# Graph attention on one core: the last half tile in three loads, and fewer dependent VectorE steps in the last group

## The reference

```python
h = input @ W
e = (h @ a1)[:, None] + (h @ a2)[None, :]
e = jnp.where(e > 0, e, ALPHA * e)
e = jnp.where(adj > 0, e, NEG)
attention = jax.nn.softmax(e, axis=1)
x = _layernorm(x + elu(attention @ h), axis=-1)
```

## Time and profile before

| | us |
|---|---|
| median of three runs | 710.41 |
| lowest, highest | 709.22, 713.4 |
| the profiled execution's own time | 709.52 |
| its span (first to last instruction) | 707.7 |
| PE, DVE, ACT, POOL busy | 549.5, 480.7, 524.2, 444.0 |
| mean granted TensorE clock | 0.894 |

### The profile page before, as it was taken

How to read it: one execution, slowest core, us unless ns; L and a number is a source line. 1 busy time by engine, 2 the same in 40 slices (tenths; PEclk the granted TensorE clock), 3 DMA queues, 4 the chain that set the end, 5 groups by cost and what they waited for, 6 DMA issues and landing times.

```text
span 707.7 us, 11837 instructions
## 1 busy us (share of the span) xinstructions
PE 549.5 (78%) x3034; PEld 343.5 (49%) x3083; DVE 480.7 (68%) x2058; ACT 524.2 (74%) x423; POOL 444.0 (63%) x676
## 2 busy tenths in 40 slices
PE   0867898686787878988987777788787877798885
PEld 0323455453455545555555454455554544565554
DVE  2374577877666676766776767766667767656886
ACT  0846778777787878787877787878787878778741
POOL 2015377776666765666776676666776676667773
PEclk9979998999999997988999999989999999878998
DMA  8999999999999999999999999999999999999645
GB/s 346 333 413 426 426 426 424 427 426 425 426 426 426 429 427 427 427 426 427 426 428 430 426 426 425 429 425 428 429 426 428 425 427 426 427 424 428 274 119 151
DMA packets 34598, 285.57 MB, mean 404 GB/s; under 512 B 5528, under 2 KB 13872, under 8 KB 18064
## 3 DMA queue, kind: packets, MB, share of 16 engines
q1 hardware_dynamic: 29024, 276.83, 93.6%
q0 software_dynamic: 5120, 8.42, 3.3%
q10 hardware_dynamic: 432, 0.07, 0.1%
HBM read 283.18 MB, written 4.19 MB: 406 GB/s over the span
## 4 chain that ended last, share of the span: by engine, by line
DMA 67%; ACT 11%; PE 10%; issue 5%; DVE 4%; POOL 1%; SPq 1%; ACTq 0%; POOLq 0%; DVEq 0%
DMA adj_sb<-in_adj 65%; ACT adj_squared L618 11%; PE fold L752 6%; DMA a_sb<-in_L_gnn_a 2%; POOL edge_row L383 1%; PE misc L794 1%; PE x_att_ps L817 1%; PE fold L748 1%; SPq L421 1%; DVE spread L395 0%; PE small L767 0%; DVE top_map L1000 0%; DVE dot L1111 0%; POOL spread L401 0%; PE x_att_ps L820 0%
## 5 line engine op out<-in xcount | busy, mean ns | idle before, releaser
L618 ACT ACTIVATE adj_squared<-adj_sb 128x4096 bf16<-128x4096 int32 x128 | 462.7, 3615 | 117.8 <-DMA adj_sb<-in_adj 116.9
L752 PE MATMUL fold<-adj_sb,bit_ident 128*128 128x512 bf16 x993 | 301.5, 448 | 9.7 <-DMA adj_sb<-in_adj 5.3
L543 POOL DMA_INDIRECT nb<-in_x,index x160 | 165.2, 1032 | 93.7 <-issue 60.4
L752 PEld LDWEIGHTS fold<-adj_sb,bit_ident 128*128 128x128 bf16 x1024 | 110.3, 108 | 154.0 <-issue 67.2
L1000 DVE MAX8 top_map<-fold 128x8 f32<-128x512 f32 x128 | 89.4, 699 | 72.4 <-PE fold L752 69.5
L748 PE MATMUL fold<-col_no,ident_bf 128*128 128x512 bf16 x112 | 47.9, 428 | 111.0 <-DMA adj_sb<-in_adj 110.8
L383 POOL TENSOR_SCALAR edge_row<-row_iota,edge_in 128x128 f32<-128x128 int32 x186 | 127.4, 699 | 0.0
L401 POOL TENSOR_TENSOR spread<-edge_row,edge_w 128x384 f32<-128x384 f32 x60 | 54.9, 934 | 83.2 <-DVE edge_w L1156 83.2
L748 PEld LDWEIGHTS fold<-col_no,ident_bf 128*128 128x128 bf16 x128 | 15.9, 124 | 133.6 <-issue 90.1
L516 POOL TENSOR_SCALAR empty_diag<-ident,counts 128x128 f32<-128x128 f32 x64 | 39.2, 618 | 54.3 <-DVE counts L1036 33.3
L817 PEld LDWEIGHTS x_att_ps<-spread,nb 128*128 128x128 f32 x372 | 52.8, 205 | 8.1 <-issue 2.3
(11 more groups left out here) (154 smaller groups left out, 615.1 us busy)
## 6 DMA issues: line engine op xcount, KB each, us to landing
adj_sb<-in_adj SPq DMA_DIRECT2D x127, 2048.0 KB, 16.2
out<-x_sb SPq DMA_DIRECT2D x2, 1536.0 KB, 7.8
nb<-in_x,index POOLq DMA_INDIRECT x160, 6.2
adj_sb<-in_adj SPq DMA_DIRECT2D x2, 1024.0 KB, 15.0
out<-x_sb SPq DMA_DIRECT2D x4, 128.0 KB, 2.8
out<-x_sb SPq DMA_DIRECT2D x1, 384.0 KB, 8.0
out<-x_sb SPq DMA_DIRECT2D x2, 64.0 KB, 1.6
W_sb<-in_L_gnn_W ACTq DMA_DIRECT2D x1, 64.0 KB, 7.9
```

Source lines behind the costliest of these rows:

```text
L543: nc.gpsimd.indirect_dma_start(out=nb_of(j, g)[:, c, :], out_offset=None, in_=x[:, :], in_offset=bass.IndirectOffsetOnAxis(ap=index[:, g, ...
L618: nc.scalar.activation(adj_squared[:, h % 2, :], adj_sb[:, h % LOAD_SLOTS, :], ACT.Square, accum_out=half_sum[:, h:h + 1]).then_inc(square ...
L752: last = nc.tensor.matmul(fold[:, h % LOAD_SLOTS, :], bit_ident[:, b, :], adj_low[:, h % LOAD_SLOTS, b * FOLD:(b + 1) * FOLD, 0], start=Fa ...
```

## The change

Three edits, all of which act in the last group alone; the loop and the other groups run the instructions of before.

1. The second part of the last half, 2048 columns, is loaded in two parts of 1024. PE waits for the one ahead of bit 4 and for the other ahead of bit 6; ACT waits for both.
2. In the last group `lists` scales the picked values by 2^8 in one instruction (`peel[0]`) beside the rounding (`top_int`), masks the exponent of that (`top_lead`) beside the column, subtracts it (`peel[1]`) beside `from_base`, and masks both peels in one instruction of 64 columns with a mask of four exponent bits. The constants of the threshold and of the row numbers are those of the new codes. One memset of one column is added at the start.
3. In the last group `scores` adds the own score and takes the minimum with `cap` in one instruction per tile, ahead of the leaky ReLU.

```diff
@@ load
-                        parts = 2 if is_final(i, g) and h == HALVES - 1 else 1
+                        cuts = LAST_CUTS if is_last_half(i, h) else (0, BITS)
...
+        LAST_CUTS = (0, BITS // 2, 3 * BITS // 4, BITS)
@@ square_half
-                        act.wait_ge(rest_loaded, 16)
+                        for landed in rest_loaded:
+                            act.wait_ge(landed, 16)
@@ fold_half
-                        if is_last_half(i, h) and b == BITS // 2:
-                            pe.wait_ge(rest_loaded, 16)
+                        if is_last_half(i, h) and b in LAST_CUTS[1:]:
+                            pe.wait_ge(rest_loaded[LAST_CUTS.index(b) - 1], 16)
@@ lists
+                    if is_final(j, g):
+                        nc.vector.tensor_scalar(peel[:, 0, :], maps, LIFT / UNIT, LIFT * (FOLD // 2), ALU.mult, ALU.add)
+                        v.after(nc.vector.tensor_scalar(top_int[:], maps, 1.0 / UNIT, float(FOLD // 2),
+                                                        ALU.mult, ALU.add))
+                        nc.vector.tensor_tensor(top_lead[:], peel[:, 0, :].bitcast(i32),
+                                                exp_bits[:, 0:1].to_broadcast(flat), ALU.bitwise_and)
+                        v.after(nc.vector.tensor_tensor(top_col[:], top_int[:], col_bits[:, 0:1].to_broadcast(flat),
+                                                        ALU.bitwise_and))
+                        nc.vector.tensor_tensor(peel[:, 1, :], peel[:, 0, :], top_lead[:].bitcast(fp32), ALU.subtract)
+                        v.after(nc.vector.tensor_tensor(from_base[:], half_base[:].rearrange("p q s -> p (q s)"),
+                                                        top_col[:], ALU.subtract))
+                        v.after(nc.vector.tensor_tensor(
+                            lead[:].rearrange("p k s -> p (k s)"), peel[:].rearrange("p k s -> p (k s)").bitcast(i32),
+                            kept_bits[:, 0:1].to_broadcast([P, PEELS * 2 * PAIR * 8]), ALU.bitwise_and))
...
-                    v.after(nc.vector.tensor_scalar(is_code[:], sent[:, :, 0:SLOTS], float(NO_CODE), None, ALU.is_gt))
+                    v.after(nc.vector.tensor_scalar(is_code[:], sent[:, :, 0:SLOTS],
+                                                    float(LAST_NO_CODE if is_final(j, g) else NO_CODE), None, ALU.is_gt))
@@ scores
+                    if is_final(j, g):
+                        for t in range(PAIR):
+                            last = nc.vector.scalar_tensor_tensor(
+                                score[:, t, :], t_row_ps[:, t, :], s_all[:, last_tile(t):last_tile(t) + 1],
+                                cap[:, g, t, :], ALU.add, ALU.min)
+                        v.after(last)
+                        v.after(nc.vector.scalar_tensor_tensor(score_l[:], score[:], ALPHA, score[:],
+                                                               ALU.mult, ALU.max))
+                        top_scores(slots)
+                        return
```

More of the change, by code:

```diff
@@ L81, in graph_attention @@
     NO_CODE = COL_0 - N - FOLD
+    LIFT = 2.0 ** 8
+    KEPT_BITS = 0b00010111 << 23
+    LAST_COL_0 = FOLD * (16 + BITS - 1) + HALF
+    LAST_NO_CODE = LAST_COL_0 - N
     EDGES = CHUNKS * P // PAIR
@@ L120, in graph_attention @@
         exp_bits = sb("exp_bits", [P, 1], i32)
+        kept_bits = sb("kept_bits", [P, 1], i32)
         half_base = sb("half_base", [P, 2 * PAIR, 8], i32)
@@ L151, in graph_attention @@
         rest_code = sb("rest_code", [P, 2 * PAIR * 8], fp32)
+        peel = sb("peel", [P, PEELS, 2 * PAIR * 8], fp32)
+        top_lead = sb("top_lead", [P, 2 * PAIR * 8], i32)
         from_base = sb("from_base", [P, 2 * PAIR * 8], fp32)
@@ L257, in graph_attention @@
         loaded = [sem(f"loaded{s}") for s in range(LOAD_SLOTS)]
-        rest_loaded = sem("rest_loaded")
+        rest_loaded = [sem(f"rest_loaded{k}") for k in range(2)]
         chunk_gathered = [sem(f"chunk_gathered{c}") for c in range(CHUNKS)]
@@ L415, in step @@
                             sp.wait_ge(folded, i * HALVES + (h + 1 - LOAD_SLOTS))
-                        parts = 2 if is_final(i, g) and h == HALVES - 1 else 1
-                        size = HALF // parts
-                        for k in range(parts):
-                            lo = (h % 2) * HALF + k * size
-                            tile = adj_tiles[bass.ds(i * BODY + h // 2, 1), :, lo:lo + size]
-                            nc.sync.dma_start(adj_sb[:, h % LOAD_SLOTS, k * size:(k + 1) * size],
+                        cuts = LAST_CUTS if is_last_half(i, h) else (0, BITS)
+                        for k, (b, end) in enumerate(zip(cuts, cuts[1:])):
+                            lo, hi = (h % 2) * HALF + b * FOLD, (h % 2) * HALF + end * FOLD
+                            tile = adj_tiles[bass.ds(i * BODY + h // 2, 1), :, lo:hi]
+                            nc.sync.dma_start(adj_sb[:, h % LOAD_SLOTS, b * FOLD:end * FOLD],
                                               tile.rearrange("o p c -> (o p) c")).then_inc(
-                                                  rest_loaded if k else loaded[h % LOAD_SLOTS], 16)
+                                                  rest_loaded[k - 1] if k else loaded[h % LOAD_SLOTS], 16)
                     if first(i) and g == 0:
@@ L958, in _ @@
                 nc.vector.memset(exp_bits[:], EXP_BITS)
+                nc.vector.memset(kept_bits[:], KEPT_BITS)
                 nc.vector.memset(col_bits[:], FOLD - 1)
@@ L1012, in lists @@
[L1012 to L1018 removed]
+                    maps = top_map[:].rearrange("p q s -> p (q s)")
@@ new lines, in lists @@
+                    if is_final(j, g):
[12 more added lines that the diff above has]
+                            kept_bits[:, 0:1].to_broadcast([P, PEELS * 2 * PAIR * 8]), ALU.bitwise_and))
+                    else:
+                        v.after(nc.vector.tensor_scalar(top_int[:], maps,
+                                                        1.0 / UNIT, float(FOLD // 2), ALU.mult, ALU.add))
+                        v.after(nc.vector.tensor_tensor(top_col[:], top_int[:], col_bits[:, 0:1].to_broadcast(flat),
+                                                        ALU.bitwise_and))
+                        nc.vector.tensor_tensor(from_base[:], half_base[:].rearrange("p q s -> p (q s)"), top_col[:],
+                                                ALU.subtract)
+                        v.after(nc.vector.tensor_tensor(top_code[:], top_int[:], top_col[:], ALU.subtract))
+                        v.after(nc.vector.tensor_tensor(lead[:, 0, :], top_code[:].bitcast(i32),
+                                                        exp_bits[:, 0:1].to_broadcast(flat), ALU.bitwise_and))
+                        v.after(nc.vector.tensor_tensor(rest_code[:], top_code[:], lead[:, 0, :].bitcast(fp32),
+                                                        ALU.subtract))
+                        v.after(nc.vector.tensor_tensor(lead[:, 1, :], rest_code[:].bitcast(i32),
+                                                        exp_bits[:, 0:1].to_broadcast(flat), ALU.bitwise_and))
```

17 lines of the change are left out of this document (3 added, 14 removed).

## The result

The changed kernel takes 721.43 us (median of 4 runs, 719.64 to 722.88), the kernel before, run beside it on the same chip, 710.40 (4 runs): a ratio of 1.0145, with a 95% interval of 1.0125 to 1.0165. The forecast was 709.6 within 708.4 to 711.3; the median lies 10.1 us over the upper bound, more than three times the width of that range.

The account below looks back on a forecast made before the run. The prediction took DMA, 67% of the span, as the bound. Its terms 0.20 + 0.21 + 0 = 0.41 us, taken as 0.4 from a middle of 710.0, gave 709.6 us, range 708.4 to 711.3.

Parts of the forecast that it names:

- the first one: Whole kernel: the loop reading `adj` stays as it is, so only the 36.9 us behind the last load can change.
- Three loads: Last half: PE runs without a stop and DVE's MAX8 loses its idle time; gain 0.16 to 0.24 us, taken 0.20.
- Rival B: PE's wait ahead of bit 6: the last part lands later, kernel 0.5 us slower at 710.5; chance 0.12.
- Lists: Last group, first instruction to `cand`: pairs without waits cut 1.46 us to 1.25, a gain of 0.21.
- rival A: VectorE pays per instruction, not per wait: `lists` stays at 1.46 us, only 0.2 us gained, 709.8; chance 0.08.
- Scores: Last group, up to the maximum: 0.64 us becomes 0.55, but hidden behind PE's sums; term 0, at most 0.1.
- What moves along: Tail: the 0.41 us passes through PE, POOL's copy (idle 0.58 us, 0.17 left) and the last gathers.
- rival D: Tail: smaller slack or a DVE wait loses 0.1 to 0.3 us, or `scores` gains 0.1; 709.5 to 709.9; chance 0.13.
- The clock: Tail: TensorE's clock falls; at half clock PE's 5.4 us of the chain double, giving 715; chance 0.02.
- same: Whole time: no change beyond the measurable 0.5% (3.6 us), chance 0.94; faster 0.03, slower 0.03.

Follow-up runs that it names:

- tiles_only: The kernel before with only the change's three new tiles declared, unused, in the changed kernel's places: 720.05 us, ratio 1.0138.
- after: The changed kernel with all three edits, against the kernel before: 721.43 us, ratio 1.0145.
- nb_32: The kernel before with a 32-byte pad ahead of `nb` and another behind, so `nb` begins 32 past a multiple of 512: 719.21 us, ratio 1.0138.
- shift_384: The kernel before with only `peel` and `top_lead` declared, unused, so `nb` begins 384 past a multiple of 512: 721.94 us, ratio 1.0153.
- no_split: The changed kernel without the three-part load; the other two edits and the new tiles stay: 719.87 us, ratio 1.0128 against the kernel before.
- before: The kernel without the change, the reference for the others: 710.40 us beside the changed kernel.
- shift_32: The kernel before with only `kept_bits` declared, unused, so `nb` begins 32 past a multiple of 512: 722.10 us, ratio 1.0174.
- nb_alone: The kernel before with 32 bytes ahead of `nb` and 480 behind, so only `nb` changes its place within 512: 720.93 us, ratio 1.0137.
- nb_256: The kernel before with a 256-byte pad ahead of `nb` and another behind, so `nb` begins 256 past a multiple of 512: 711.36 us, ratio 1.0005.
- adj_only: The kernel before with `adj_sb` and `nb` on multiples of 512, `x_sb` left 128 past one: 707.24 us, ratio 0.9950.
- all_512: The kernel before with `x_sb`, `adj_sb` and `nb` all on multiples of 512: 703.56 us, ratio 0.9898.
- after_aligned: The changed kernel with a 96-byte pad putting `nb` back on a multiple of 512: 709.22 us, ratio 0.9977 against the kernel before.
- best: The changed kernel with `x_sb`, `adj_sb` and `nb` all on multiples of 512: 702.08 us, ratio 0.9881 against the kernel before.
- split_only: The kernel before with only the last half loaded in three parts: 711.32 us, ratio 1.0016.
- tiles_last: The changed kernel with its three new tiles declared behind all others: 710.58 us, ratio 1.0003 against the kernel before.
- again: The changed kernel run once more, unaltered: 720.00 us, ratio 1.0118 against the kernel before.

## Why the prediction was wrong

**The step that failed** is the first one: "The middle of the kernel is the reading of `adj`, and the change leaves the loop as it is, so only the stretch behind the last load can change." The instructions of the loop were left, but not the addresses that they write to. `tiles_only` has not one instruction more than the kernel before and costs 1.0138. The stretch that the prediction dismissed holds 9 us of loss, some twenty times the 0.41 that it worked out with care elsewhere. It had also priced what the change adds in instructions, DMAs and a memset, and never the declarations, which the excerpt of the diff ahead of it leaves out.

**Three loads:** 0.16 to 0.24 forecast. Shown where PE comes ahead of the landing, and nothing where it comes late. In `after` DVE, from the first of the two MAX8 on (timeline):

```profile
684.79 1.28 DVE L1011 MAX8 top_map<-fold 128x8 f32<-128x512 f32 x2
686.11 0.29 DVE L1019 TENSOR_SCALAR peel<-top_map 128x32 f32<-128x32 f32 x1
686.21 0.22 DVE L1020 TENSOR_SCALAR top_int<-top_map 128x32 int32<-128x32 f32 x1
686.46 0.19 DVE L1022 TENSOR_TENSOR top_lead<-peel,exp_bits 128x32 int32<-128x32 int32 x1
686.57 0.18 DVE L1024 TENSOR_TENSOR top_col<-top_int,col_bits 128x32 int32<-128x32 int32 x1
...
687.12 0.22 DVE L1029 TENSOR_TENSOR lead<-peel,kept_bits 128x64 int32<-128x64 int32 x1
687.37 0.23 DVE L1046 SCALAR_TENSOR_TENSOR cand<-lead,from_base 128x64 f32<-128x64 int32 x1
```

The two MAX8 now follow each other with no idle time, 1.28 us in all; before, they took from 671.09 to 672.64, 1.55. But in `after` PE came to the last half when all of it had landed, and kernels without the split in which PE came late as well have 1.28 too: `nb_32` and `shift_384`, which have no edit at all, and `no_split`:

```profile
681.37 1.28 DVE L1011 MAX8 top_map<-fold 128x8 f32<-128x512 f32 x2
```

So there the gain is not the split's. Where PE opens the last half 0.9 to 1.1 us ahead of the last packet's end, the two MAX8 take 1.45 to 1.57 without the split (`before`, `tiles_only`, `shift_32`, `nb_alone`, `nb_256`, `adj_only`, `all_512`) and 1.28 with it (`after_aligned`, `best`). Both kernels show the forecast mechanism, PE's eight products in one piece with no wait (`after_aligned` here):

```profile
669.33 1.97 PE L763 MATMUL fold<-adj_sb,bit_ident 128*128 128x512 bf16 x8
```

Part of it is given back at once: behind two MAX8 with no wait between them the first instruction of `lists` lasts 0.29 us where it lasted 0.18, and the old chain then takes 1.56 (`nb_32`) or 1.57 (`split_only`, below) and not 1.46. The prediction had no such term. Rival B, the later landing, did not happen: no kernel with the split has a wait of PE in the last half.

```profile
672.96 1.29 DVE L1001 MAX8 top_map<-fold 128x8 f32<-128x512 f32 x2
674.28 0.29 DVE L1007 TENSOR_SCALAR top_int<-top_map 128x32 int32<-128x32 f32 x1
```

**Lists:** 1.25 us forecast from the first instruction to `cand`; 687.37 - 686.11 = 1.26 above, and 1.26 in `no_split`, `tiles_last` and `after_aligned` as well, 1.27 in `again`. `best` has 1.45, because its first pair took 0.48 and 0.41 us and not 0.29 and 0.22; why is not known. Pairs start 0.10 and 0.11 apart. With the old chain it is 1.57 in `split_only` and 1.45 in `nb_256` and `all_512`. Under like conditions, two MAX8 with no wait ahead, the gain is thus 1.57 - 1.26 = 0.31 and not 0.21. The rule of the Trainium skill (page "VectorE: DVE Perf Modes", section "The DRAIN you can't avoid") that removing waits gains nothing, rival A, does not hold for these small instructions: eight instructions before and after, 1.46 or 1.57 against 1.26. The section also says that a next instruction that is not held starts earlier, and with that the trace agrees: 0.10 and 0.11 us behind the other where a step with a wait takes 0.22.

**Scores:** 0.55 us forecast, 0.60 measured (0.61 in `after_aligned`, 0.73 in `tiles_last`), as from the pair of reads from PSUM to the next step it is 0.39 and not 0.33. PE's sums follow on one another in `after_aligned` with no gap ahead of `small<-share`, so the 0.04 gained there is hidden, as said.

**What moves along.** From the opening of the last half to the first of the last gathers it was 681.77 - 669.36 = 12.41 us; in `after_aligned` it is 681.14 - 669.11 = 12.03, so 0.38 arrives there. The split has little part in it: it is 12.03 in `no_split` as well, and 12.34 in `split_only` against 12.33 to 12.41 in the kernels without any edit. POOL's copies stand at 678.01 and 678.14 with no idle time between, where there were 0.58 us: the slack was used up entirely, not down to 0.17.

```profile
678.01 0.20 POOL L535 COPY half_sum_all<-half_sum 128x4 f32<-128x4 f32 x1
678.14 0.19 POOL L541 COPY counts_all<-counts 128x4 f32<-128x4 f32 x1
...
681.14 1.06 POOL L553 DMA_INDIRECT nb<-in_x,index  x1 [1.25 <-DVE index L1131]
```

To the end of the span it is 707.0 - 669.11 = 37.89 us against 38.34: 0.45 gained, forecast 0.41; in `after` it is 37.95. These two are the best cases. In `again`, `no_split` and `best`, whose clock stayed at 1.00 in this stretch too, it is 38.21, 38.28 and 38.30, hardly less than the 38.27 to 38.35 of the kernels without any edit and with a full clock in the tail. The last gathers start as early in `again` and `no_split` as in `after`, and the gain is lost behind them, where DVE comes to the scores of the group ahead and waits for PE's `send_scores`. That wait is in these three, and neither in `after` and `after_aligned` nor in the kernels without any edit; first `after_aligned`, then `best`:

```profile
684.48 0.15 DVE L1172 TENSOR_TENSOR score<-misc,s_all 128x20 f32<-128x20 f32 x1
```

```profile
677.52 0.18 DVE L1173 TENSOR_TENSOR score<-misc,s_all 128x20 f32<-128x20 f32 x1 [0.17 <-PE misc L806]
```

From the opening of the last half this instruction starts at 15.37 us in `after_aligned` and at 15.61 to 15.72 in the three. So rival D, a gain that does not arrive, did happen, in three of the five executions that have the edits to `lists` and `scores` and a full clock in the tail, and at a wait that the prediction had not named; PE's products for it start at the same 13.66 to 13.76 us in all five, and what makes DVE wait for them in some is not known. `tiles_last` has the same 12.02 us up to that gather (683.11 - 671.09), but 38.71 to the end of its span: its clock fell once more, to 0.71 over 680 to 685 us, and there six products from `spread` take 1.53 us where they take 0.94.

So the forecast of the tail was right in the mechanisms on DVE. That its 0.41 came out in two executions is in part luck: `lists` gave more than its term, the split less, and what arrives at the end depends on a wait outside the sum. It is too small to be shown by times: 0.9977 (0.9961 to 0.9993) for `after_aligned` is the most that can be said for it, and `tiles_last` has 1.0003.

**The clock** was given 0.02, because "PE's work behind the load is the same". The fall came ahead of the last halves, a place that this argument leaves out. What it cost here (4.3 us in `after`, some 2.4 in the tail of `all_512` and of `nb_256`, 0.5 to 0.8 in that of `tiles_last`) shows that a chance for it belonged in the range on the upper side. It falls in kernels without any edit as well, so it scatters every measurement here and does not come from the edits alone.

**The chances** had 0.94 on "same" because every case considered lay in the tail. No rival said that the change might touch the loop after all. A ratio of 1.0145 with an interval of 1.0125 to 1.0165 is beyond the 0.5% that the prediction took for the limit of what can be told apart, on the slower side, to which it gave 0.03.

## Why a place costs time

Three numbers from the runs can be put side by side. `nb` takes 160 gathers of 128 rows, 20480 rows of 512 bytes. Off a multiple of 256 it costs 720.93 - 711.32 = 9.6 us of 16 engines (`nb_alone`), 7.5 ns of one engine per row. `x_sb` takes 8192 rows of 512 bytes, and 128 off it costs 707.24 - 703.56 = 3.7 us, 7.2 ns per row. `adj_sb` takes 16384 rows of 16 KB, and 128 off it costs 711.29 - 707.24 = 4.1 us, 4.0 ns per row. So it is a price per row that does not grow with the row's length, and it does not grow with the distance from the multiple either (32, 384 and 416 are alike). These are estimates, worked out from differences of medians. The packets' own records bear them out: for `x_sb` (116.5 - 88.5) / 4 = 7.0 ns per row, and for `adj_sb` a packet over 1 us away from any gather's takes 614.2 ns in `after_aligned` and 611.4 in `best`, 2.8 ns per row.

The Trainium skill has a rule that fits (page "DMA: Bandwidth & Descriptors", section "How a descriptor splits into AXI transactions"): a transfer is cut at 256-byte boundaries, so one that does not begin on such a boundary needs one piece more. By it a row of 512 bytes goes from two pieces to three wherever between two boundaries it begins, and a row of 16 KB from 64 to 65. The runs agree in both: one price for 32, 384 and 416, none for 256. They agree less in the beats that the section counts, 16 for the aligned row and by its way of counting 17, 20 and 21 for 32, 384 and 416 past: the runs do not tell these three apart. The section speaks of reads, and here it is the writes that are off; that the cut is the cause is argued from this fit and not shown. Tried were 32, 128 and 160 bytes past a multiple of 256, and none; other places, and rows of other lengths, were not.

## What to carry to other kernels

A declaration is a part of a change: whatever stands behind a new tile moves, and if the target of a small-row transfer is among it, the kernel can lose 1.4% of its time with no instruction changed, as here, where the DMA engines are full. Put new tiles last, or pad so that targets of transfers begin on a multiple of 256 bytes, and compare the GB/s of the untouched stretch before reading anything else. And before saying that a stretch cannot change, ask what it shares with the rest: addresses, engines and the clock.

## What the runs showed of the hardware that was not expected

- The place of a transfer's target within SBUF counts: 427 against 421 GB/s for 32 bytes (`nb_alone`), and 429 with all targets on multiples of 512.
- The cost of the gathers' place appears in the records of the other stream: 16-KB packets of `adj` are 644 ns long in place of 617 while the badly placed gathers fly, and unchanged outside, while the share of the gathers' own queue in such a round is 10.0% in both.
- The first instruction of `lists`, of 32 columns on VectorE, behind two MAX8 with no wait between them lasts 0.29 us (`split_only`) where it lasts 0.18 when the second MAX8 had waited (`before`).
- The granted clock of TensorE fell to 0.50 somewhere in the last 65 us of the span in every traced kernel, for 3 to 14 us (its last 5 us left aside), but at different places, and only some cost time: 666 to 680 us in `after` (4.3 us lost), 678 to 685 in `all_512` and 686 to 692 in `nb_256` (2.4 us lost in each), 655 to 662 in `tiles_only` and 646 to 653 in `before` (nothing to be seen). What decides the place is not known.
